# A ternary feed-forward layer whose rows are turned by DMA transposes, and two edits in a sparse expert layer

## The reference, cut to what matters

```
def bitlinear(x, w):
    xn = layer_norm(x)
    x_hat = absmax_quant(xn)          # clip to +-(128 - 1e-6)/128 of the row's largest magnitude
    w_hat = ternarize_weights(w)      # -1, 0, +1 times one scale
    return einsum('bsd,od->bso', x_hat, w_hat)
h = bitlinear(x, w_fc)                # 512 -> 2048
h = gelu(h, approximate=False)
y = bitlinear(h, w_proj)              # 2048 -> 512; then X = layer_norm(X + y)
```

## Time and profile before

| | |
|---|---|
| median of 3 runs | 2095.75 us |
| the profiled execution, its own time | 2098.51 us |
| its span, first to last instruction | 2096.7 us |
| mean granted TensorE clock | 0.93 of full speed |
| busy over the span | PE 80%, DVE 70%, ACT 48%, POOL 27% |
| ternary phase, first to last DVE instruction | 774.75 to 1104.42 us |
| sparse phase, first to last gate_hi | 1601.8 to 1956.1 us |

### The profile page before, as it was taken

The page is one execution under the profiler, slowest core; times in us unless marked ns, Lnnn a source line. Parts: engine busy times, 40 slices in busy tenths (PEclk is TensorE's granted clock), DMA queues, the critical chain, the costliest instruction groups (busy, mean ns, idle before and its releaser), DMA issues. The chain is left out here.

```text
span 2096.7 us, 35409 instructions
## 1 busy us (share of the span) xinstructions
PE 1678.1 (80%) x13401; PEld 864.9 (41%) x13401; DVE 1463.9 (70%) x2115; ACT 997.4 (48%) x1549; POOL 571.1 (27%) x568
## 2 busy tenths in 40 slices
PE   0579999777999858888984977974696888888697
PEld 0353333344333223444441543543463555555364
DVE  3558998446898478999963364364624999999667
ACT  4345777434677713333333222222133777777532
POOL 0250000252000033344321122123261444444255
PEclk9889999998999989999996988996798999999899
DMA  8000000000000000000002000002004665345234
GB/s 298 1 2 2 2 2 2 1 1 1 2 2 2 2 1 1 1 0 0 1 1 91 1 1 1 1 1 96 32 2 144 195 195 153 113 154 183 94 102 139
DMA packets 49393, 105.96 MB, mean 51 GB/s; under 512 B 7096, under 2 KB 10392, under 8 KB 48720
## 3 DMA queue, kind: packets, MB, share of 16 engines
q1 hardware_dynamic: 37632, 75.99, 10.4%
q0 software_dynamic: 7424, 21.00, 3.9%
q10 hardware_dynamic: 4176, 6.82, 0.9%
HBM read 149.68 MB, written 21.01 MB: 81 GB/s over the span
## 5 line engine op out<-in xcount | busy, mean ns | idle before, releaser
L624 ACT ACTIVATE attn_prob<-attn_ps_t 128x512 f32<-128x512 f32 x576 | 312.6, 595 | 127.9 <-PE attn_ps_t L591 126.3
L643 DVE TENSOR_REDUCE attn_mx<-attn_ps_s 128x2 f32<-128x1024 f32 (+3 forms) x304 | 342.8, 1163 | 41.5 <-PE attn_ps_s L572 38.0
L136 PE MATMUL sparse_ps_g<-sparse_wg,sparse_xT 128*128 128x352 f16 x1152 | 190.5, 316 | 54.7 <-DVE sparse_xT L1900 54.7
L604 PE MATMUL attn_ps_o<-attn_prob,V 128*32 128x256 f32 x2304 | 174.8, 389 | 3.6 <-ACT attn_prob L624 2.7
L1905 DVE SCALAR_TENSOR_TENSOR sparse_wg<-sparse_raw_g,sparse_wg 128x2816 f16<-128x2816 f32 x48 | 148.4, 3092 | 37.9 <-ACT sparse_wg L1857 37.8
L136 PEld LDWEIGHTS sparse_ps_g<-sparse_wg,sparse_xT 128*128 128x128 f16 x1152 | 107.8, 99 | 128.8 <-DVE sparse_xT L1900 77.7
L778 POOL TENSOR_TENSOR wo_o<-O,wo_o 128x512 f16<-128x512 f32 (+1 forms) x16 | 18.4, 1153 | 496.0 <-ACT wo_o L750 495.9
L1942 POOL TENSOR_TENSOR sparse_h<-sparse_hid,sparse_h 128x352 f16<-128x352 f32 x48 | 87.7, 1826 | 217.4 <-ACT sparse_h L1876 217.4
L1021 PE MATMUL lin_ps_z<-w,lin_xT 128*128 128x512 f16 x576 | 136.2, 387 | 0.0
L1857 ACT ACTIVATE sparse_wg<-sparse_raw_g 128x2816 f16<-128x2816 f32 x48 | 122.0, 2541 | 17.2 <-DMA sparse_raw_g<-in_L_ffn_w_gate_up_dram 17.2
L849 PE MATMUL ffn_ps_fc<-wfcT,ffn_xT 128*128 128x512 f16 x512 | 123.6, 393 | 8.1 <-DVE ffn_xT L926 8.1
(11 more groups left out here) (320 smaller groups left out, 3407.2 us busy)
## 6 DMA issues: line engine op xcount, KB each, us to landing
sparse_raw_g<-in_L_ffn_w_gate_up_dram SPq DMA_DIRECT2D x48, 1408.0 KB
sparse_raw_d<-in_L_ffn_w_down_dram SPq DMA_DIRECT2D x48, 512.0 KB
y_d<-sparse_y SPq DMA_DIRECT2D x48, 256.0 KB, 3.6
sparse_raw_d<-in_L_ffn_w_down_dram SPq DMA_DIRECT2D x48, 192.0 KB
prep_w_fc<-in_L_ffn_w_fc_dram SPq DMA_DIRECT2D x4, 1024.0 KB, 15.6
X<-in_L_attn_x_dram ACTq DMA_DIRECT2D x1, 4096.0 KB, 39.6
prep_w_proj<-in_L_ffn_w_proj_dram SPq DMA_DIRECT2D x4, 1024.0 KB, 22.4
x_d<-route_x SPq DMA_DIRECT2D x16, 256.0 KB, 2.0
```

The lines of the kernel that those rows point to most:

```text
L136: last = pe.matmul(out, a(k), b(k), start=(k == 0 and n == 0), stop=(k == chunks - 1 and n == 2))
L604: last = pe.matmul(ps_o[32 * jj:32 * jj + 32, 256 * half:256 * half + 256], V[:, kt, 4 * jg + jj, :], prob[(2 * q + jj // 2) % 4][:, half, ...
L624: act.activation(prob[g % 4][:, par, :, :], ps_t[:, (2 * g + par) % 3, :, :], ACT.Exp, scale=HD ** -0.5).then_inc(exp_done, 1)
L643: dve.tensor_reduce(mx[x % 2][:, c, :, at:at + per], ps_s[:, 2 * (r % 2):2 * (r % 2) + 2, 0:per * n].rearrange("p e (h k) -> p e h k", k=n ...
```

## The change

In the ternary phase all steps are written out instead of looped. The transposes leave PE: SP issues three DMA transposes per tile from SBUF to SBUF, one for xT (128 x 1024 numbers of 16 bits, 256 KB) and one for each part of hT (128 x 2048, 512 KB each). With them go the PSUM tensors ps_x and ps_h and all copies out of them (x_evac and the four turns on ACT and DVE). The freed PSUM gives ps_y two buffers. The low parts xlo and hlo are made by DVE instead of POOL. The normalisation of h goes from DVE to ACT, as an activation with scale rstd and bias shift = -mean * rstd; DVE makes -mean (back), POOL the product (shift). The lags change.

In the sparse phase hlo goes from POOL to DVE, between xevac and down_lo, and on ACT hhi stands ahead of down_hi instead of behind it.

The core of the diff:

```
             @block.sync
+                def xt(t):
+                    u = t % 2
+                    sp.wait_ge(xh_done, t + 1)
+                    sp.wait_ge(xl_done, t + 1)
+                    after(sp, fc_done, (t - 1) * NB)
+                    sp.dma_start_transpose(out=xT[u][:, :, :, :].rearrange("p a k c -> p (a k) c"),
+                                           in_=x2[u][:, :, :].rearrange("p a n -> p (a n)")).then_inc(xt_in[u], 16)
+                def ht(part):
+                    def fn(t):
+                        u = t % 2
+                        sp.wait_ge(hl_done if part else hh_done, t + 1)
+                        after(sp, y_done, t - 1)
+                        sp.dma_start_transpose(out=hT[u][:, part, :, :], in_=h2[u][:, part, :]).then_inc(ht_in[u][part], 16)
+                unrolled(NT, [(3, xt), (5, ht(0)), (5, ht(1))])
             PE:
-                run_tiles(pe, NT, [(4, of(fc, 0)), (7, of(ht, 0, 1)), (4, of(fc, 1, 2)), (7, of(ht, 2, 3)),
-                                   (4, of(fc, 3)), (3, xt), (7, proj)])
+                unrolled(NT, [(4, fc), (6, proj)])
             ACT:
+                def h_norm(t):
+                    act.wait_ge(shift_done, t + 1)
+                    after(act, hl_done, t - 1)
+                    act.activation(hn[u][:, :], h[u][:, :, :].rearrange("p n k -> p (n k)"), ACT.Identity,
+                                   scale=ln_h.rstd[u][:, :], bias=shift[u][:, :]).then_inc(hn_done, 1)
-                run_tiles(act, NT, [(7, evacuate(act, copy, ht_evac_a, 0)), (4, gelu(0, 1)),
-                                    (7, evacuate(act, copy, ht_evac_a, 2)), (4, gelu(2, 3)), (2, xhi), (6, hhi)])
+                unrolled(NT, [(4, gelu(0, 1)), (5, hhi), (4, gelu(2, 3)), (2, xhi), (4, h_norm)])
             DVE:
-                run_tiles(dve, NT, [(6, h_norm), (9, norm), (8, residual), (7, turn(1)), (5, h_stats), (7, turn(3)),
-                                    (3, x_evac), (1, x_norm), (0, x_stats)])
+                unrolled(NT, [(5, h_clip), (8, norm), (7, residual), (5, hlo), (1, x_norm), (4, h_stats), (2, xlo), (0, x_stats)])
             POOL:
+                def h_root(t):
+                    u = t % 2
+                    after(pool, hn_done, t - 1)
+                    pool.wait_ge(ln_h.s_var, t + 1)
+                    pool.tensor_tensor(ln_h.rstd[u][:, :], ln_h.var[u][:, :], m.minus_half[:, :], ALU.pow).then_inc(ln_h.s_rstd, 1)
+                    pool.wait_ge(back_done, t + 1)
+                    pool.wait_ge(ln_h.s_rstd, t + 1)
+                    pool.tensor_tensor(shift[u][:, :], back[u][:, :], ln_h.rstd[u][:, :], ALU.mult).then_inc(shift_done, 1)
+                unrolled(NT, [(7, lambda t: ln_r.root(pool, t, t % 2)), (4, h_root), (0, lambda t: ln_x.root(pool, t, t % 2))])
@@ sparse phase, ACT, DVE, POOL
-                unrolled(NG, [(1, gate_hi), (2, tanh), (3, hevac), (2, down_hi), (2, hhi), (3, yevac)])
+                unrolled(NG, [(1, gate_hi), (2, tanh), (3, hevac), (2, hhi), (2, down_hi), (3, yevac)])
-                unrolled(NG, [(1, gate_lo), (2, swiglu), (1, xevac), (2, down_lo)])
+                unrolled(NG, [(1, gate_lo), (2, swiglu), (1, xevac), (2, hlo), (2, down_lo)])
-                unrolled(NG, [(0, gather), (2, hlo)])
+                unrolled(NG, [(0, gather)])
```

More of the change, by code:

```diff
@@ new lines, in ternary_ffn, with _ @@
+        hh_done, hl_done, y_done, r_done = f.sems("hh_done hl_done y_done r_done")
+        xt_in = [f.sem(f"xt_in{u}") for u in range(2)]
+        ht_in = [[f.sem(f"ht_in{u}{part}") for part in range(2)] for u in range(2)]
+        with f.block() as block:
+            @block.sync
+            def _(sp):
+                def xt(t):
[11 more added lines that the diff above has]
+                        sp.dma_start_transpose(out=hT[u][:, part, :, :], in_=h2[u][:, part, :]).then_inc(ht_in[u][part], 16)
+                    return fn
+                unrolled(NT, [(3, xt), (5, ht(0)), (5, ht(1))])
@@ L835, in _, with fc @@
             @block.tensor
             def _(pe):
[L837 to L845, removed]
+                def fc(t):
+                    u = t % 2
+                    pe.wait_ge(xt_in[u], 16 * (t // 2 + 1))
+                    for n in range(NB):
@@ L848, in fc @@
                             for part in range(2):
-                                last = pe.matmul(ps_fc[n][:, :], xT[u][:, part, k, :],
-                                                 m.wfcT[:, k, n * D:(n + 1) * D],
+                                last = pe.matmul(ps_fc[n][:, :], xT[u][:, part, k, :], m.wfcT[:, k, n * D:(n + 1) * D],
                                                  start=(k == 0 and part == 0), stop=(k == KC - 1 and part == 1))
                         last.then_inc(fc_done, 1)
[L854 to L868, removed]
+                def proj(t):
+                    u = t % 2
+                    after(pe, r_done, t - 1)
                     for part in range(2):
+                        pe.wait_ge(ht_in[u][part], 16 * (t // 2 + 1))
                         for k in range(NK):
-                            last = pe.matmul(ps_y[:, :], hT[u][:, part, k, :], m.wprojT[:, k, :],
+                            last = pe.matmul(ps_y[u][:, :], hT[u][:, part, k, :], m.wprojT[:, k, :],
@@ L901, in gelu, with xhi, hhi @@
                     return fn
-                def hhi(t, u):
+                def xhi(t):
+                    u = t % 2
+                    act.wait_ge(q_x.s_clipped, t + 1)
+                    after(act, xt_in[u], 16 * (t // 2))
+                    act.activation(x2[u][:, 0, :], xn[u][:, :], ACT.Copy).then_inc(xh_done, 1)
+                def hhi(t):
+                    u = t % 2
                     act.wait_ge(q_h.s_clipped, t + 1)
-                    after(act, ht_done, t * 4 - 4)
+                    after(act, ht_in[u][0], 16 * (t // 2))
```

98 lines of the change are left out of this document (40 added, 58 removed).

## The result

The change made the kernel slower: 2134.14 us (median of four runs, 2131.85 to 2136.97) against 2095.45 us for the kernel before on the same chip (four runs, 2093.37 to 2096.2). The ratio is 1.0187, with an interval of 1.0169 to 1.0205. The forecast was 2140.

The account below looks back on a forecast made before the run. Sparse was taken as bound by a ring of DVE and ACT waiting for each other, ternary by DVE. 2098.5 (profiled) + 68.5 sparse - 25 ternary = 2142, stated as 2140 after allowing for the median; range 2112 to 2230.

Parts of the forecast that it names:

- ring of starts: Sparse phase: gate_lo, swiglu, hhi, yevac, gate_hi, waiting for each other across DVE and ACT, set the step of 7.56 us.
- Term 1.49 per step: Sparse phase, ACT: the two down_hi instructions, put between hhi and yevac, lengthen each step from 7.56 to 9.05 us.
- Sum 68.5: Sparse phase: groups 2 to 47 pay for down_hi, 46 x 1.49 = 68.5 us lost.
- Rival B: Sparse phase: down_hi fits where ACT waits, only the ternary gain stays; 2071 us, at best 2045; chance 10%.
- hlo on DVE, sparse, was priced at nothing: Sparse phase: hlo's about 0.45 us falls where DVE waits; 21 us if the ring were not the bound.
- The ternary tile: Ternary phase: DVE work 15.0 plus waits 1.6, 0.3 and 0.55 make 17.5 us per tile, from 19.1.
- priced at 1.6 + 0.3: Ternary phase, DVE: h_clip waits 1.6 us for ACT's normalisation, 0.3 more because POOL's root waits behind xlo.
- The 18.0 us: Ternary phase: time per tile with all of the port lock between DVE and POOL; 16.6 without the port.
- the 11 taken for the run-out: End of ternary phase: 11 us gained, 3.7 from the collision, 2.4 from slow proj, the rest from idle and copies.
- about 10 us a tile: Ternary phase: assumed cost of the DMA transposes, between 7.6 and 12.8, under the tile's 17.5.
- rival A: Ternary phase: DMA transposes are the bound; 2180 us at 20 per tile, 2269 at 25.6; chance 17%, 5% beyond 2300.
- rival C: Ternary phase: gaps let PE fall to 1.2 GHz; at half clock throughout 28 us per tile, 2307 us; chance 5%.

Follow-up runs that it names:

- order_alone: The kernel before with one edit alone: on ACT in the sparse phase hhi stands ahead of down_hi; 2163.19 us, ratio 1.0326.
- order_back: The changed kernel with one edit undone: on ACT in the sparse phase down_hi stands ahead of hhi again; 2062.71 us, ratio 0.9851.
- sparse_hlo_alone: The kernel before with only the sparse hlo moved from POOL to DVE; 2095.73 us, ratio 0.9998.
- transposes_twice: The changed kernel with each DMA transpose of the ternary phase issued a second time into tensors nobody reads; 2130.54 us, ratio 1.0163.
- cover_order_back: The changed kernel with ternary x_norm behind h_stats on DVE and sparse down_hi ahead of hhi on ACT again; 2039.91 us, ratio 0.9736.
- yevac_first: The changed kernel with x_norm behind h_stats and, on ACT in the sparse phase, down_hi and yevac both ahead of hhi; 2033.71 us, ratio 0.9706.

## Why the prediction was right

**The mechanism.** It read the sparse phase as a ring of starts and found the moved pair inside it. Term 1.49 per step: measured 1.87 - 0.40 = 1.47. Sum 68.5: measured 67.4 in the trace, 67.8 by order_alone, 71.4 by order_back (67.2 of it in the phase). The signs that it named came: gate_lo 9.03 us apart, ACT idle 3.04 ahead of hhi, DVE waiting 0.94 for down_hi. Rival B, that down_hi fits where ACT waits, was wrong for the reason given: ACT's wait comes ahead of hhi, and the pair stood behind it.

**hlo on DVE, sparse, was priced at nothing** and cost nothing: sparse_hlo_alone has the ratio 0.9998 (0.9989 to 1.0008).

**The ternary tile was the term that was off**, 17.5 against 16.82. DVE's own work was priced at 15.0 and measured 14.93 (16.82 - 1.89). The wait was priced at 1.6 + 0.3 and measured 1.89, partly by luck, as errors cancel in it: ACT's normalisation takes 2.09, not 1.90, POOL's root beside xlo 0.92 where 0.85 was counted, and the product on POOL 0.19, not 0.55. The step that failed is the last: "behind hlo, delays x_norm by one root (0.55)". POOL's root did wait behind hlo, 2.63 instead of 0.55, but x_norm took its 0.54 and started 2.21 after hlo did: DVE never waited.

The Trainium skill, "SBUF — State Buffer", section "SBUF: two separate sides", has the port pair of DVE and GpSimd locked for a whole instruction, also for two SBUF inputs. The trace agrees for POOL (2.63 behind hlo, 0.92 beside xlo). The 18.0 us that I drew from it, with DVE paying in turn, is what the trace refutes for x_norm behind this root. DVE does pay elsewhere: the 1.34 of L1923 in before, shown under sparse_hlo_alone, is the row for two inputs that the prediction said it lacked. Why the one was spared and the other not, no run shows.

From the third to the twelfth maximum of h the nine tiles take 151.3 us instead of 172.8, a gain of 21.5 where the prediction had 14. The other 11.4 of the 32.9 look like the 11 taken for the run-out, but that is luck. From the last maximum to the end after takes 22.9 against 29.4, a gain of 6.5, and the four tiles before it gain 0.9. The start, counted at nothing, gives 4.1: the first maximum comes 28.3 us after the phase's first DVE instruction instead of 32.3. The sum by measured terms is 2098.5 + 67.4 - 32.9 + 3.9 = 2136.9. The prediction's 2142 was 1.1 too high in the sparse phase and 7.9 in the ternary; the 3.9 outside both, for which it had no term, hid half of that. So the time came closer than the ternary sum deserved.

**Transposes.** The choice of about 10 us a tile was close enough: 39.5% of 16 engines over 315 us is 7.8 us a tile. The packets are small (84,824 for 23.7 MB in these 315 us, 280 bytes each), yet they cost less than a tile. PE waits for hT 19.8 us in 13 times. The prediction had named such a wait as the sign of A, and the sign was wrong: in transposes_twice PE waits 57.8 us in all for xT and hT, where after has 36.4, and the time per tile stays. The Trainium skill, "VectorE: DVE Perf Modes", section "The three transpose paths", gives 1309 ns for a 128x128 block; 40 of them one after another were the estimated 52 us. Here a tile's 40 blocks fit in 16.82 us twice over, so that figure is no price per block in a row. (The 840 us that the prediction gave the phase for it left out the fill and run-out of 25 that rival A's other sums have.)

**PE's clock** (rival C) was 0.96 and 1.00 in the two windows, as before. Over the ternary phase it was 0.91 (770 to 1085 us) where before had 0.95 (770 to 1105). In the steady tiles DVE never waits for PE, so it costs nothing there; what it costs in the run-out, where DVE waits 7.9 us for PE, was not separated.

## What to carry to other kernels

Where no engine is full, look for two engines that wait for each other in every step, write down the starts between two equal instructions, and see whether they add up to the step: here what was put inside that ring cost its whole time (1.47 us a step), and what was put where the ring waits cost nothing. The average shares of busy time did not tell these two places apart. When work moves to another engine, count the cover between the hand-over and the instruction that waits; here one exchange of two stages removed the wait and was worth more than moving the work back.

## What the runs showed of the hardware

The gather on POOL (an indirect DMA) ends 0.81 to 0.83 us after DVE's gate_lo, an instruction with two SBUF inputs, whenever it begins inside it. That holds for 44 of the 48 gathers in each of the nine versions without hlo on POOL (the other four of each do not begin inside one), though they begin 0.5 to 2.7 us into gate_lo and take from 1.18 to 3.40. In after:

```profile
1726.45 3.39 POOL L1946 DMA_INDIRECT sparse_xg<-x_d,token  x1 [5.63 <-PE sparse_ps_x L1815]
```

gate_lo ran 1725.93 to 1729.02, the gather ended at 1729.84. In cover_order_back it ran 1702.14 to 1704.07 with gate_lo ending at 1703.25; in yevac_first 1707.36 to 1709.35, and 1708.53. Before, where it began 0.9 us ahead of gate_lo, it took 1.24; in order_alone, clear of gate_lo, 0.97. In the steady steps nobody waited for it. That gate_lo holds it up is inferred from these ends; no run moved the gather alone. The Trainium skill, "SBUF — State Buffer", section "SBUF: two separate sides", tells of the like: while DVE runs an instruction in a mode that uses both of its port pairs, GpSimd can't write the descriptors of a DMA that it issues. The page says so of such modes; that an instruction with two inputs does the same is what these rows suggest.

A transpose of 256 KB occupied SP for 1.23 us in the steady tiles and landed in 3.1 (median). One of 512 KB occupied it for 1.7 to 3.5, median 1.9, and landed in 4.4. At twice the traffic hT still landed in 4.5.
